# Reordering a software-pipelined step over four engines: another order of the full step of an RWKV-7/MoE kernel, and a first step in which the mixes wait for one tanh

## The reference

```python
xn = layernorm(x)
dx = shift(xn) - xn                         # the token before, minus this one
mix = tanh((xn + dx * x_miu) @ x_A)         # 6 groups of 32
r_in, w_in, k_in, v_in, a_in, g_in = xn + dx * (lambdas + mix @ x_B)
r, v = r_in @ rW.T, v_in @ vW.T
g = tanh(g_in @ g_A) @ g_B
w = -softplus(-(w_miu + tanh(w_in @ w_A) @ w_B)) - 0.5
k = normalise(k_in @ kW.T + tanh(k_in @ k_A) @ k_B)
a_gate = 2 * sigmoid(a_time + a_in @ a_A @ a_B)
y = wkv7(r, w, kk, v, -k, k * a_gate)       # state S of 64 x 64 a head, 4 heads, 2048 steps
s = (groupnorm(y) + bonus(r, k, v)) * g @ oW.T
f = MoE(xn)    # relu(xn @ wi + bi + rank-16 expert term) @ wo for the top 2 of 8 experts
out = x + s * silu(f)
```

## Time and profile before

| | |
|---|---|
| device time, median of 3 runs | 993.99 us (992.45 to 994.77) |
| the profiled execution | 991.9 us |
| its span, first to last instruction | 989.7 us |
| TensorE matmuls busy | 975.6 us, 99% of the span |
| VectorE, ScalarE, GpSimd busy | 84%, 64%, 45% |
| TensorE clock granted | 1.000 throughout |

### The profile page before, as it was taken

One profiled execution on the slowest core, in us unless ns is written; L12 is line 12 of the kernel. 1 busy time (PEld: TensorE's weight loads), 2 busy tenths in 40 slices (PEclk: granted clock), 3 DMA queues, 4 the chain that ended last, 5 costly groups with the idle time before them and its releaser, 6 DMA issues.

```text
span 989.7 us, 46754 instructions
## 1 busy us (share of the span) xinstructions
PE 975.6 (99%) x20570; PEld 769.4 (78%) x20570; DVE 835.0 (84%) x1684; ACT 635.2 (64%) x1481; POOL 442.0 (45%) x537
## 2 busy tenths in 40 slices
PE   8999999999999999999999999999999999999997
PEld 5777778787787877778877787877878777787775
DVE  5887979889798897979979798797988979789776
ACT  3665666656657566675666666566575665756655
POOL 3461734537244371634617345272442715436150
PEclk9999999999999999999999999999999999999999
DMA  7000000000000000000000000000000000000000
GB/s 261 13 3 3 3 4 23 4 24 4 4 24 4 23 5 23 3 4 23 4 24 4 3 25 3 23 4 3 24 4 24 3 25 3 3 24 4 13 4 23
DMA packets 9416, 17.28 MB, mean 17 GB/s; under 512 B 1920, under 2 KB 4224, under 8 KB 8960
## 3 DMA queue, kind: packets, MB, share of 16 engines
q1 hardware_dynamic: 9216, 14.30, 4.4%
HBM read 10.10 MB, written 4.19 MB: 14 GB/s over the span
## 4 chain that ended last, share of the span: by engine, by line
PE 96%; ACT 2%; DVE 1%; issue 1%; ACTq 0%; DVEq 0%
PE bank L255 34%; PE bank L254 20%; PE grams L470 10%; PE bank L348 5%; PE bank L485 3%; PE bank L496 3%; PE grams L539 2%; PE grams L444 2%; PE grams L594 2%; PE grams L559 2%; PE bank L570 2%; PE bank L363 2%; PE bank L529 2%; PE bank L379 2%; PE bank L580 1%; PE bank L303 1%
## 5 line engine op out<-in xcount | busy, mean ns | idle before, releaser
L1265 POOL TENSOR_TENSOR bk<-bk,tot 128x256 f32<-128x256 f32 x192 | 155.1, 815 | 137.1 <-PE grams L470 137.1
L1583 DVE COPY_PREDICATED gm<-c_mask_g,grams 128x1024 f32<-128x1024 int32 x96 | 161.4, 1681 | 6.1 <-PE grams L470 4.3
L1021 ACT ACTIVATE gl<-gm 32x128 f32<-32x128 f32 x320 | 99.1, 310 | 79.1 <-DVE gm L1583 72.9
L1246 POOL TENSOR_TENSOR xd<-mtmp,xnc 128x512 f32<-128x512 f32 x96 | 122.3, 1275 | 14.4 <-DVE mtmp L1449 12.6
L914 ACT ACTIVATE relu<-bank,prm 128x256 f32<-128x256 f32 x256 | 105.6, 471 | 36.1 <-PE bank L255 33.6
L470 PEld LDWEIGHTS grams<-ar,bk 64*64 64x64 f32 x6144 | 102.0, 134 | 19.8 <-issue 14.8
L255 PE MATMUL bank<-w_wo,hid 128*128 128x256 f32 x488 | 116.1, 386 | 0.0
L470 PE MATMUL grams<-ar,bk 64*64 64x64 f32 x6144 | 110.2, 220 | 0.0
L1593 DVE TENSOR_TENSOR ar<-ar,tot 128x512 f32<-128x512 f32 x96 | 92.3, 962 | 13.2 <-PE grams L470 13.2
L255 PEld LDWEIGHTS bank<-w_wo,hid 128*128 128x128 f32 x488 | 90.2, 190 | 13.1
L255 PE MATMUL bank<-xnc,w_wi 128*128 128x256 f32 x392 | 94.4, 384 | 0.9 <-ACT relu L914 0.9
(11 more groups left out here) (241 smaller groups left out, 2149.0 us busy)
## 6 DMA issues: line engine op xcount, KB each, us to landing
x_in<-x SPq DMA_DIRECT2D x16, 256.0 KB, 2.8
out<-out_t SPq DMA_DIRECT2D x15, 256.0 KB, 2.0
w_wi<-w_wi_dram SPq DMA_DIRECT2D x1, 1024.0 KB, 6.8
w_wo<-w_wo_dram SPq DMA_DIRECT2D x1, 1024.0 KB, 8.8
w_lora_B<-w_lora_B_dram SPq DMA_DIRECT2D x1, 512.0 KB, 7.6
w_x_B<-w_x_B_dram SPq DMA_DIRECT2D x1, 384.0 KB, 3.2
w_kW<-w_kW_dram SPq DMA_DIRECT2D x1, 256.0 KB, 3.8
w_rW<-w_rW_dram SPq DMA_DIRECT2D x1, 256.0 KB, 4.3
```

Source lines behind the costliest of these rows:

```text
L1021: A(gl[l % 2][o:o + 32, :, :, :].rearrange("p q g (c n m) -> p (q g c) n m", c=2, m=m), right(gm[o:o + 32, :, :, :, b, 0, 32 * k:32 * k + ...
L1246: tt(xd[:, q, :, :], mtmp[:, k % 2, :, :], xnc[steps["front"] % 2][:, :, :], ALU.add).then_inc(S(f"xd_{k}_done"), 1)
L1265: tt(v, v, d, ALU.mult).then_inc(S(f"bk{k}_scaled"), 1)
L1583: run(v.copy_predicated(dst, msk.to_broadcast([128, 32, HALF // m, m]), src), "g_stored")
```

## The change

The same work is done on the same data; only orders, the PSUM banks (`USED_BY`, `FIRST_USED_BY`) and the places of some waits differ.

**Step 1.** `miu(0)` waits for one tanh (`mixt_done` 1) and no longer for all five. `miu(1)` writes banks 0 and 2 and follows at once; `mtmp` has four places and no longer two. One of the six sums is moved from GpSimd to VectorE (`mixed_sum(0)`). `wk_A` comes ahead of `kW`; on ScalarE the tanhs come ahead of `exps`, `sig_` ahead of `kraw_`, and `nrm_` ahead of `ha` and `agate_`.

The core of the diff (step 1 on TensorE and ScalarE, then parts of the full step):

```diff
+        def mixes_in(pair):
+            return (bank[0], bank[2]) if steps["front"] == 0 and pair == 1 else MIU
...
             def miu(pair):
-                pe.wait_ge(*till("mixt_done", 5))
+                pe.wait_ge(*till("mixt_done", 5 if pair == 1 else 1))
...
+                        warm(2)
+                        mix()
                         warm(1)
-                        mix()
-                        warm(2)
                         miu(0)
-                        warm(3)
+                        pe.wait_ge(*till("xnc_done", 1))
+                        pe.wait_ge(*till("route_read", 1))
+                        miu(1)
+                        warm(2)
                         pe.wait_ge(*till("mx_0_done", 2))
                         pe.wait_ge(*till("mx_1_done", 2))
-                        miu(1)
+                        miu(2)
+                        wk_A()
                         kW(half=True)
-                        wk_A()
...
                         rt_e()
+                        mixt_e()
+                        mixt_f()
                         exps()
-                        mixt_e()
                         hwk()
+                        sig_()
+                        kraw_()
                         hg()
-                        kraw_()
+                        nrm_()
                         ha()
-                        sig_()
+                        gate_(step)
+                        r_e()
                         agate_()
-                        nrm_()
-                        r_e()
-                        gate_(step)
```

More of the change, by code:

```diff
@@ L757, in tile @@
                     if rec:
-                        diff(0, half=True)
                         base(3, half=True)
+                        gram(2)
                     if front:
@@ L766, in tile @@
                     if rec:
-                        gram(2)
                         inv_x(1)
-                        base(2)
+                        diff(0)
                         lora(3)
                         inv_off(1)
+                        gram(3)
+                        inv_x(2)
+                        base(2)
                     if front:
@@ L776, in tile @@
                     if rec:
-                        gram(3)
-                        inv_x(2)
+                        gram(4)
+                        inv_off(2)
+                        lora(2, half=True)
                     if front:
@@ L782, in tile @@
                     if rec:
-                        lora(2, half=True)
-                        inv_off(2)
+                        inv_x(3)
                     if front:
                         pe.wait_ge(*till("mx_2_done", 2))
[L787 to L793, removed]
                         kW()
                     if rec:
-                        inv_x(3)
+                        inv_off(3)
                     if front:
-                        pe.wait_ge(*till("mx_5_done", 2))
+                        pe.wait_ge(*till("hwk_done", 1))
                         wk_B()
                     if rec:
-                        inv_off(3)
                         gram(5)
+                        down(0, first=True)
                         inv_x(4)
@@ L806, in tile @@
                         pe.wait_ge(*till("ksq_done", 1))
-                        g_A()
+                        pe.wait_ge(*till("sig_done", 2))
+                        miu(2)
+                    if rec:
+                        inv_off(4)
+                        rec_p(0)
+                        top_x()
+                        diff(3)
                     if post:
                         if front:
-                            pe.wait_ge(*till("sig_done", 2))
+                            pe.wait_ge(*till("mx_4_done", 2))
                         elif full:
@@ L814, in tile @@
                     if rec:
[L815 to L820, removed]
+                        top_off()
+                        if front:
+                            pe.wait_ge(*till("mx_5_done", 2))
+                        elif full:
+                            pe.wait_ge(*till("gate_done", 0))
+                        keys_to_tokens(0)
                         if post:
@@ L873, in tile @@
                     if rec:
[L874 removed]
+                        rec_p(1)
                     if front:
[L876 to L881 removed]
+                        pe.wait_ge(*till("nrm_done", 1))
+                        r_()
                     if rec:
[L883 to L884 removed]
+                        rec_sa(1)
+                        y_state(1)
                     if front:
@@ L1786, in tile @@
                         bn()
-                    if rec:
-                        scale_ar(0)
-                    if front:
                         xn_()
@@ L1792, in tile @@
                         store(0)
+                        scale_ar(0)
                     if front:
```

356 lines of the change are left out of this document (173 added, 183 removed).

## The result

The changed kernel takes 1006.27 us (median of 4 runs, 1004.74 to 1007.77), the kernel before 993.64 on the same chip: a ratio of 1.0127, 95% interval 1.0115 to 1.0140. It is slower by 12.6 us, where 991.2 was forecast.

What follows compares the result with a forecast made beforehand. TensorE was taken as the bound, busy 975.6 of 989.7 us, so a step costs its list plus waits. Terms: -3.9 - 0.75 - 1.6 + 3.5 = -2.75 us, 993.99 to 991.2 us; range 985.5 to 999.

Steps and rivals of the forecast that it cites:

- The gram chain: VectorE's list up to `gram(4)` and `gram(5)`: inputs ready 0.5 and 0.45 us ahead, so costed at nothing.
- A full step: Period of one full step: 60.07 + 0.05 - 0.10 + 0.25 + 0.05 = 60.32 us, so +3.5 us over 14 steps.
- the slower rival: `scale_ar(4)` comes late through exclusive meetings with `mixed`, so `gram(5)` waits 0.8 us a step: 1002.4 us, chance 0.2.
- Array shapes, +0.05: TensorE's full step: 36 shape changes before and after, slightly different kinds, about +0.05 us a step.
- gram(4), -0.10: Wait ahead of `gram(4)` in the full step goes, as `scale_bk(3, k)` runs ahead of every `mixed`: -0.1 us a step.
- +0.05 of small things: `rec_sa(0)` behind `inv_last` and `norm` behind `keys_out(0)`, within 0.1 us of their inputs: +0.05 us a step.
- rec_y(1), +0.25: New TensorE wait for `sa_out` at `rec_y(1)`, 1.32 us of cover for 1.50: 0.25 us a step.
- Table loads at nothing: ScalarE: seven table loads a full step for five, 2.56 us more in its queue, nothing on the path.
- Issue stalls, -1.6: TensorE's stalls inside `inv_x(4)` in four full steps shrink because `down(0)` breaks the run of small products: -1.6 us.
- Step 2, -0.75: The `bkt` wait goes, -1.3 us, plus 0.25 for `rec_y(1)` and 0.3 for `r_`: -0.75 us.
- Step 1, -3.9: Earlier `miu(0)` and `wk_B`, 1.9 us, plus 1.3 and 0.8 in front of `nrm_`: -3.9 us taken.
- Step 17 at nothing: Step 17: no change, forecast 0 us.

Runs made afterwards that it cites:

- repaired order: Changed kernel with `bv_` back early on GpSimd, `bonus_e` ahead of `diag_store`, and `down(1)` in half form ahead of `rec_y(1)`: 993.08 us, ratio 0.9997.
- the swap: Changed kernel with `bonus_e` ahead of `diag_store` on VectorE in steps 2 to 16: 1001.93 us, ratio 1.0076.
- `bv_` early: Changed kernel with GpSimd's `bv_` moved from the end of steps 2 to 16 back behind `scale_bk(1, 1)`: 994.28 us, ratio 0.9996.
- the repaired versions: Changed kernel with `bv_` moved back, alone or with `down(1)`, `bonus_e` and `ysg_` moves added: 994.28, 1000.99, 997.81 and 993.08 us.

## Why the prediction was wrong

The step that failed is the layout of VectorE's list under "**The gram chain**": "I cost this at nothing; the cover is that slack". At `gram(4)` and `gram(5)` that was right. But I laid the list end to end only up to there, and so "A full step" has no term for what comes behind: 60.32 us was forecast and 61.50 measured, and 1.17 of it went when `bv_` was moved back. The second half, from `o_read` to `bonus_e`, has the same exclusive instructions and a GpSimd neighbour that the change brings there (`bv_`), and I priced neither; what TensorE waits for there is `bonus_e`, 1.11 us late in every full step. The mechanism was in the text ("the two engines' tensor_tensor instructions exclude one another"), and even as the slower rival, but in the wrong half of the step: 1.11 us a step in the tail, nothing at `gram(4)` and `gram(5)`. The rival's time, 1002.4, was nearer than the forecast, for a reason that it did not give.

The Trainium skill (GPSIMD Engine Reference, "1. Specifications") says that the contention is with VectorE instructions "in a 2-port perf mode or with two SBUF inputs", and names no operation. The runs agree: `dg` is a scalar_tensor_tensor, and the small copy_predicated of line 1610 went from 0.45 to 1.52 us. My text had narrowed it to tensor_tensor.

Point by point:
- *Array shapes, +0.05; gram(4), -0.10; +0.05 of small things*: not told apart, but their sum is. The repaired order has 60.07 us for 60.08 before, so together they are about nothing. Of the `gram(4)` term 0.05 can be read: from the `miu` ahead of it to `gram(4)` it is 0.96 us before and 0.91 after.
- *rec_y(1), +0.25*: right, 0.24. It came back in full once the bonus was in time and no change of shape was added; what it is worth while the bonus is late was not told apart.
- *Table loads at nothing*: right, 28 loads fewer changed nothing.
- *Issue stalls, -1.6*: right in this execution, -1.5, and in part by luck: with the same TensorE program the full steps of the swap hold 7.4 us (some 1.7 of it by the clock) and those of `bv_` early 3.3. That `down(0)` breaks the run of small products is supported by the run in which `down(1)` does so, with the new wait in it as said. But the changed order has other such places (`lora(2)`, `inv_off`), and the repaired versions show 2 to 6 us of stalls. What makes those longer when TensorE's program is the same as in the changed kernel stays open.
- *Step 2, -0.75*: -1.3. The wait for `bkt` went as said; of the 0.3 us ahead of `r_` only 0.1 came. The bonus is in time there; VectorE has less to do in that step (no `o_read`).
- *Step 1, -3.9*: -3.4. `miu(0)` at 12.04 and `wk_B` at 18.92 for 12.2 and 19.0. The root of `nrm_` came 3.96 us earlier too (23.66 for 27.62), but VectorE took it up only at 24.65, 3.39 earlier than before. It was held by
```profile
22.07 2.32 DVE L1485 TENSOR_TENSOR xmask<-rt,oh 128x256 f32<-128x256 f32 x2
```
which takes 0.76 us in a full step of the kernel before and here meets two instructions of GpSimd. The half microsecond is the same error, in step 1.
- *Step 17 at nothing*: +1.0, a stall that was not priced.

## What to carry to other kernels

When two engines exclude one another, a list must be laid out for both, over the whole step, and every instruction that is moved counts in the half that it comes into as well as in the half that it leaves. A wait that ends on another engine can take up what is saved or lost ahead of it, as the wait for the bonus took up 0.07 us: price each wait, and begin with the one that ends last. And before a group is put in as cover, look at three things: the shape of its neighbours, what it was the cover of in its old place, and what hangs on the group that it delays.

## What the runs showed of the hardware

- GpSimd and VectorE hold each other up where they meet: `hidden` 1.77 us for 0.69, `oh` on 16 columns 1.02 for 0.16, a copy_predicated within SBUF 1.52 for 0.45, while GpSimd's own `bv` goes from 1.05 to 1.49.
- Which of two colliding instructions goes first can change from step to step of one program, with starts that differ by 35 ns at most and do not tell the cases apart: its steps take 60.07 or 60.86 us. Its runs go from 988 to 997 us; in the slowest, 2.7 us of that lie in step 17, where the granted clock was 0.5 for 6.8 us.
- TensorE's issue stalls come at one and the same place in every 256 instructions, which is a packet of 16.4 KB (48 of 48 stalls), and mostly where it meets small products: half a packet more in step 1 moved those in `inv_x(4)` to other steps, a whole packet did not.
- The granted clock fell to 0.5 for 3.4 us behind an issue stall of 2.14 us, and for 6.9 us in step 1 when tiny products had run for 3.7 us.
- A group of 1.73 us between groups of another array shape costs 1.92 to 1.93, 0.2 us more; between groups in the half form the group ahead of it took 0.1 us more as well.
